# First layer: t1 and t6 turned into the score bank, and other places for copies, statistics, layer norm and loads

## The chip, the core and the metric

One Trainium2 chip, of which the kernel uses one core. The metric is the device time of one execution of the program in microseconds, the median of several executions. Names of the engines: PE is TensorE, DVE is VectorE, ACT is ScalarE, POOL is GpSimd, SP is SyncE, which only issues DMAs here.

## What is computed

Two layers over x, 128 rows of 256 tokens of 256 channels in f32. Each layer adds to x an attention over the 256 tokens of each row, on a group normalisation of its input. Cut to what matters:

```python
# layer 0
def _L0_conv_ref(x1d, x2d, norm_w, norm_b, qkv_w, x2d_w, gate_w, gate_b, final_w, final_b):
    c, h = 32, 8
    x = _layernorm(x1d, norm_w, norm_b)
    qkv = (x @ qkv_w.T).reshape(*x.shape[:-1], c, 3 * h)
    q, k, v = (qkv[..., :h], qkv[..., h:2 * h], qkv[..., 2 * h:])
    aff = jnp.einsum('bmich,bmjch->bmijh', q, k)
    gate = jax.nn.sigmoid(x @ gate_w.T + gate_b).reshape(*x.shape[:-1], c, h)
    bias = x2d @ x2d_w.T * (1.0 / math.sqrt(c))
    weights = jax.nn.softmax(aff + bias[:, None], axis=-2)
    out = jnp.einsum('bmrch,bmirh->bmich', v, weights) * gate
    return out.reshape(*x.shape[:-1], c * h) @ final_w.T + final_b
x = x + _L0_conv_ref(_gn(x), ...)      # _gn: group norm, 32 groups, over all rows and tokens
# layer 1: 4 heads of 64, only keys with |i - j| <= 16
x = x + _L1_conv_ref(_gn(x), ...)
```

## The kernel before

A prologue reads all of x once for the statistics of the first group norm (gstat0) and works out the pair bias for all rows (neg_bias). Then layer 0 runs row by row (`body0` of each engine), a second group norm follows (`group_norm(1, gstat1)`, from statistics of the rows' results), and layer 1 runs row by row (`body1`).

Each engine has its own program, written out by hand, in which the pieces of several rows stand between each other: m is the row whose softmax is finished, nxt = m + 1 the row whose projections are made, far = m + 2 the one whose normalised tokens are transposed, ahead = m + 3 the one whose tokens are scaled by the group norm, last = m - 1 the one whose heads are mixed with v, done = m - 2 the one whose result is added to x. There is no scheduler; the order of the calls in a body is the order on that engine, and semaphores tie the engines together. `over_rows` writes the first and last rows out and runs the rest in a loop of 4 rows an iteration.

A row of layer 0 on PE: the projections q, k, v and gate (12 matmuls each, since a product of f32 is made of three products of high and low parts), two groups of `scores` of four heads (24 each), eight `turns(h)` (four transposes each, of a head's 256 x 256 weights), `mixes` (32), the transposes of xn (L561), and the y projection (12). The four banks of `score` hold the scores of four heads at a time; `turn` is one bank. `turns(3)` and `turns(7)` go to the first score bank, the other six to `turn`, and each turn waits until the copy of the one before it in its bank is done.

A head's way: `scores` on PE; `mins` on DVE (L926) adds the bias and finds the row's minimum; `exps` on ACT (L722), with the sum; `inverse` on DVE (L932), for two heads at a time; `norms(r, j)` on POOL (L364) for heads 2j and 2j + 1, two instructions a head; `turns` on PE (L527); `turn_copy` to probT, on ACT (L728) for even heads, on DVE (L937) for odd ones; `mixes` on PE.

A row's tokens: SP loads x_tok (L329), POOL multiplies by the group norm's scale (L386, g_tok) and adds its shift (L392), DVE takes statistics (`bn_stats`, L1001, L1008) and ln_neg, ln_var (L1010, L1011), POOL works out ln_rstd, ln_off and xn (L370, L372, L377), PE transposes it, ACT writes xnT (L741) and the high part of src (L746), DVE its low part (`split_low`, L915: both inputs in SBUF). In the same way q, k and the attention's result have a high part from ACT (L732, L751, L757) and a low part from DVE (L952, L973, L981; the last has both inputs in SBUF). The result y is added to x on DVE (L948, y_sb) and stored by SP (L321). y_sb has two slots, and in every second row DVE takes `bn_stats` of both slots, for each of the two channel blocks (L1018).

## Time and profile before

| what | value |
|---|---|
| median of 3 runs | 3655.28 us (3653.41 to 3656.13) |
| profiled execution | 3664.15 us, its span 3662.3 us |
| PE / DVE / ACT / POOL busy over the span | 3372.3 / 3002.9 / 2776.3 / 2177.9 us |
| granted TensorE clock, mean | 0.969 |
| layer 0's loop | from about 250 to 2350 us |
| layer 1's loop | from about 2450 us to the end |

A busy time is a sum over stages with different limits, so the layer that the diff touches is read by itself. PEld is the weight load of each matmul; it has the clearer starts, and a piece's time is read from the start of its first weight load to the start of the next piece's. The other engines' operations overlap a little at their ends, so their pace too is read from start to start. Instructions with read-outs of accumulators stand beside `mins` and `exps` and overlap them.

### The profile page before, as it was taken

What the parts mean: (1) busy time and instruction counts of PE and PEld (TensorE: products, weight loads), DVE (VectorE), ACT (ScalarE), POOL (GpSimd) and SP (SyncE); (2) the same over time, 40 slices, a digit from 0 to 9 for tenths busy, and PEclk for the clock granted to TensorE, in tenths of its full rate; (3) what the DMA queues carried; (4) which work ended last, traced back from release to release, by engine and by line L of the source; (5) the groups of instructions that cost most, each with busy time, mean ns of one, the idle gap of its engine ahead of it and who ended that gap; (6) DMA issues with size and microseconds to landing.
All of it is one profiled execution on the core that took longest, in us unless ns stands there. A gap on an engine that the chain in (4) does not pass through costs nothing.

```text
span 3662.3 us, 122873 instructions
## 1 busy us (share of the span) xinstructions
PE 3372.3 (92%) x36747; PEld 3007.4 (82%) x36747; DVE 3002.9 (82%) x10850; ACT 2776.3 (76%) x8999; POOL 2177.9 (59%) x4107
## 2 busy tenths in 40 slices
PE   4459999999999999999999999799999999999999
PEld 1148888888888888888888888699999999999998
DVE  4458988888888888888888888688888888888887
ACT  1148888988888888888888988567667677776776
...
GB/s 341 349 100 54 46 49 51 44 52 45 50 52 43 52 46 48 52 43 52 46 48 50 44 52 44 30 53 52 52 52 52 52 53 54 53 52 52 52 52 47
DMA packets 189032, 238.42 MB, mean 65 GB/s; under 512 B 11824, under 2 KB 176176, under 8 KB 184752
## 3 DMA queue, kind: packets, MB, share of 16 engines
...
q8 instruction: 29, 0.48, 0.1%
...
## 4 chain that ended last, share of the span: by engine, by line
PE 58%; ACT 14%; issue 11%; DMA 6%; DVE 6%; POOL 2%; DVEq 1%; SPq 1%; ACTq 1%; POOLq 0%
PE work L477 24%; ACT prob L722 7%; PE work L486 7%; PE turn L527 5%; PE score L617 5%; PE mix L650 4%; DMA x_chunk<-xT 4%; PE mix L539 3%; PE score L505 3%; DMA x_tok<-x_nat 3%; PE turn L634 3%; ACT xnT L741 2%; ACT probT L728 2%; PE turn L635 2%; PE turn L636 2%
## 5 line engine op out<-in xcount | busy, mean ns | idle before, releaser
L364 POOL TENSOR_SCALAR prob<-prob,row_inv 128x256 f32<-128x256 f32 x2048 | 1068.0, 540 | 206.1 <-DVE row_inv L932 204.9
L722 ACT ACTIVATE prob<-prob,row_min 128x256 f32<-128x256 f32 x2048 | 1028.1, 507 | 128.3 <-DVE row_min L926 123.6
L477 PE MATMUL work<-src,w 128*128 128x256 f32 x7680 | 1067.5, 288 | 10.4 <-DVE src L915 6.7
L477 PEld LDWEIGHTS work<-src,w 128*128 128x128 f32 x7680 | 951.0, 189 | 12.3 <-DVE src L915 7.4
L415 POOL TENSOR_SCALAR prob<-prob,row_inv 128x160 f32<-128x160 f32 x1024 | 391.0, 401 | 767.4 <-DVE row_inv L1042 767.4
L926 DVE CUSTOM_DVE_ANT_0 prob<-score,neg_bias 128x256 f32<-128x256 f32 x2048 | 749.5, 417 | 17.2 <-PE score L505 10.1
L527 PE MATMUL turn<-ident,prob 128*128 128x128 f32 x3072 | 484.8, 280 | 120.0 <-ACT probT L728 101.4
L789 ACT ACTIVATE prob<-prob,row_min 128x160 f32<-128x160 f32 x1024 | 431.4, 426 | 141.7 <-DVE row_min L1035 141.6
L527 PEld LDWEIGHTS turn<-ident,prob 128*128 128x128 f32 x3072 | 336.3, 141 | 233.2 <-ACT probT L728 125.6
L477 PE MATMUL work<-att,wf 128*128 128x256 f32 x3072 | 432.1, 290 | 4.4 <-DVE att L981 3.0
L486 PE MATMUL work<-w,src 128*128 128x256 f32 x3072 | 425.8, 288 | 0.0
L722 ACT ACTIVATION_READ_ACCUMULATOR prob<-prob,row_min 128x1 f32 x2048 | 397.5, 194 | 0.0
L477 PEld LDWEIGHTS work<-att,wf 128*128 128x128 f32 x3072 | 385.0, 191 | 5.1 <-DVE att L981 3.5
L486 PEld LDWEIGHTS work<-w,src 128*128 128x128 f32 x3072 | 380.6, 189 | 0.1
L728 ACT COPY probT<-turn 128x512 f32<-128x512 f32 x512 | 297.2, 580 | 76.4 <-PE turn L527 69.8
L386 POOL TENSOR_TENSOR g_tok<-x_tok,gn_row 128x512 f32<-128x512 f32 x128 | 164.5, 1285 | 189.0 <-DMA x_tok<-x_nat 181.9
L1035 DVE CUSTOM_DVE_ANT_0 prob<-score,band 128x160 f32<-128x160 f32 x1024 | 263.3, 321 | 16.5 <-issue 2.4
L505 PE MATMUL score<-kT,nqT 32*128 32x256 f32 x6144 | 251.9, 294 | 6.1 <-DVE probT L937 3.2
L539 PE MATMUL mix<-probT,v_sb 128*32 128x256 f32 x4096 | 250.3, 385 | 0.0
L505 PEld LDWEIGHTS score<-kT,nqT 32*128 32x128 f32 x6144 | 199.7, 184 | 44.3 <-DVE probT L937 14.3
L932 DVE RECIPROCAL row_inv<-row_sum 128x4 f32<-128x4 f32 x512 | 90.2, 176 | 142.3 <-ACT prob L722 135.6
L1052 DVE SCALAR_TENSOR_TENSOR kT<-work,vec_sb,kT 128x256 fp32r<-128x256 f32 x256 | 112.1, 480 | 108.8 <-ACT kT L813 108.8
...
## 6 DMA issues: line engine op xcount, KB each, us to landing
...
x_tok<-x_nat SPq DMA_DIRECT2D x128, 256.0 KB, 3.3
x_sb<-xT SPq DMA_DIRECT2D x128, 256.0 KB, 3.4
x1T<-y_sb SPq DMA_DIRECT2D x128, 256.0 KB, 2.2
x_sb<-x1T SPq DMA_DIRECT2D x128, 256.0 KB, 2.9
outT<-y_sb SPq DMA_DIRECT2D x128, 256.0 KB, 2.2
...
```

Of the source, the lines that this page charges most:

```text
L364: pool.tensor_scalar(prob[:, h, ib], prob[:, h, ib], row_inv[:, h, ib:ib + 1], 1.0, ALU.mult, ALU.mult).then_inc(norm_done[0], 1)
L415: pool.tensor_scalar(w, w, row_inv1[:, r.base % 2, g, a, ib:ib + 1], 1.0, ALU.mult, ALU.mult).then_inc(norm_done[1], 1)
L477: ins = pe.matmul(out[:, cb], w[:, of_w, kb, cols + cb * P:cols + (cb + 1) * P], x[:, of_x, kb], start=n == 0, stop=n == len(terms) - 1)
L486: ins = pe.matmul(out[:, tb], x[:, of_x, kb, tb * P:(tb + 1) * P], w[:, of_w, kb, cols:cols + CH], start=n == 0, stop=n == len(terms) - 1)
L505: ins = pe.matmul(score[:, h, ib], nqT[q, r.base % 2, of_q, hg, ib * P:(ib + 1) * P], kT[q, r.base % 2, of_k, hg], start=n == 0, stop=n == ...
L527: ins = pe.transpose(to[:, jb * TOK + ib * P:jb * TOK + (ib + 1) * P], prob[:, h, ib, jb * P:(jb + 1) * P], ident[:])
L539: ins = pe.matmul(mix[h * D0:(h + 1) * D0, hg], v_sb[:, r.base % 2, jb, c:c + D0], probT[:, hg, h, jb], start=jb == 0, stop=jb == TB - 1, ...
L722: act.activation(prob[:, h, ib], prob[:, h, ib], ACT.Exp, bias=row_min[:, h, ib:ib + 1], scale=-1.0, accum_out=row_sum[:, h, ib:ib + 1]).t ...
L728: act.copy(probT[:, h // HPG, h % HPG].rearrange("p b t -> p (b t)"), turn[:]).then_inc(turn_done[0][0], 1)
L789: act.activation(w, w, ACT.Exp, bias=row_min1[:, m.base % 2, g, a, ib:ib + 1], scale=-1.0, accum_out=row_sum1[:, m.base % 2, g, a, ib:ib + ...
L926: dve.tensor_tensor_reduce(prob[:, h, ib], score[:, h % HPG, ib], neg_bias[:, ib, h], 1.0, 3.0e38, ALU.add, ALU.min, row_min[:, h, ib:ib + ...
L1035: dve.tensor_tensor_reduce(prob1[:, m.base % 2, g, a, ib * WIN:(ib + 1) * WIN], score[:, 2 * g + a, ib, 0:WIN], band[:, ib], 1.0, 3.0e38, ...
```

## The change

On each engine the same instructions are issued for a row, with the same sizes. What differs is the bank of two turns, the waits that follow from that, and the order.

- PE: turns 1, 3 and 6 go to the score bank, the others, 7 too, to `turn`. Turn 1 stands right behind turn 0, turn 6 behind turn 5 and ahead of the y projection. The waits in `turns` and `scores` follow.
- ACT: exponentials of head 5 right behind copy 0; those of heads 6, 7 and copy 4 ahead of the high part of att; the copy of v, the gate and copy 6 ahead of the next row's heads 0 to 2.
- DVE: the minima of head 7 behind the copy of turn 1; those of the next row's heads 0 and 1 ahead of att's low part, those of 2 and 3 and the inverse behind the statistics of g; copy 7 last. The statistics of y_sb are split: block 1 at the head of even rows, block 0 in the middle of odd ones, and the last one behind the loop.
- POOL: the norms of heads 4, 5 ahead of both operations on g; layer norm of row m + 3 at the end of the body, ahead of the norms of the next row's heads 0 and 1, in place of that of m + 2 at its start.
- SP: the load of x_tok ahead of the store of y and the load of x_sb.

The diff, cut to its core (waits of the moved pieces stay as they were, but for layer norm's far, which becomes ahead):

```diff
                     last, far, ahead = m + -1, m + 3, m + 4
+                    if n == 0 and ahead.exists:
+
+                        wait(sp, gn_scaled, ahead.times(1, -1))
+                        apart(sp, sp_passed)
+                        sp.dma_start(x_tok[:, ahead.base % 2], x_tok_v[:, bass.ds(ahead.times(TB), TB), :]
+                                     ).then_inc(x_tok_in[ahead.base % 2], 16)
                     if last.exists:
...
@@ -364,20 +364,9 @@
                             pool.tensor_scalar(prob[:, h, ib], prob[:, h, ib], row_inv[:, h, ib:ib + 1],
                                                1.0, ALU.mult, ALU.mult).then_inc(norm_done[0], 1)
...
-                if far.exists:
-                    wait(pool, ln_var_done, far.times(2, 2))
-                    apart(pool, pool_passed)
-                    pool.tensor_tensor(ln_rstd[:], ln_var[:], minus_half[:], ALU.pow).then_inc(ln_rstd_done, 1)
-                    wait(pool, ln_rstd_done, far.times(2, 1))
...
                 if m.exists:
                     norms(m, 1)
+                    norms(m, 2)
                 if ahead.exists:
 
                     wait(pool, x_tok_in[ahead.base % 2], ahead.times(16, 16, of=2))
...
                     pool.tensor_tensor(g, x_tok[:, ahead.base % 2], gn_row[:, 0].unsqueeze(1).broadcast_to([P, TB, CH]),
                                        ALU.mult).then_inc(gn_scaled, 1)
-                if m.exists:
-                    norms(m, 2)
-                if ahead.exists:
                     wait(pool, gn_scaled, ahead.times(1, 1))
                     pool.tensor_tensor(g, g, gn_row[:, 1].unsqueeze(1).broadcast_to([P, TB, CH]), ALU.add
                                        ).then_inc(g_done[0], 1)
                 if m.exists:
                     norms(m, 3)
+                if ahead.exists:
+                    wait(pool, ln_var_done, ahead.times(2, 2))
...
                 if nxt.exists:
                     norms(nxt, 0)
...
-                    wait(pe, turn_done[0][1], r.times(PAIRS0, 2 * hg - 2))
+                    if hg == 0:
+                        wait(pe, turn_done[0][1], r.times(PAIRS0, -2))
+                    else:
+                        wait(pe, turn_done[0][0], r.times(PAIRS0, 0))
...
                 def turns(h):
                     wait(pe, norm_done[0], m.times(TB * H0, TB * (h + 1)))
                     to = turn[:]
-                    if h % HPG == HPG - 1:
+                    if h in (1, 3, 6):
 
                         to = score[:, 0].rearrange("p b t -> p (b t)")
-                        if h < HPG:
-                            wait(pe, min_done[0], m.times(TB * H0, TB * (HPG + 1)))
-                        elif nxt.exists:
+                    if h == 0:
+                        wait(pe, turn_done[0][1], m.times(PAIRS0, 0))
+                    elif h == 1:
+                        wait(pe, min_done[0], m.times(TB * H0, TB * (HPG + 1)))
+                    elif h == 2:
+                        wait(pe, turn_done[0][0], m.times(PAIRS0, 1))
+                    elif h == 3:
+                        wait(pe, turn_done[0][1], m.times(PAIRS0, 1))
+                    elif h == 4:
+                        wait(pe, turn_done[0][0], m.times(PAIRS0, 2))
+                    elif h == 5:
+                        wait(pe, turn_done[0][0], m.times(PAIRS0, 3))
+                    elif h == 6:
+                        wait(pe, turn_done[0][1], m.times(PAIRS0, 2))
+                        if nxt.exists:
                             wait(pe, min_done[0], nxt.times(TB * H0, TB))
-                    elif h % HPG == 0:
-                        wait(pe, turn_done[0][0], m.times(PAIRS0, h // 2))
-                    elif h % HPG == 1:
-                        wait(pe, turn_done[0][0], m.times(PAIRS0, h // 2 + 1))
                     else:
-                        wait(pe, turn_done[0][1], m.times(PAIRS0, h // 2))
+                        wait(pe, turn_done[0][1], m.times(PAIRS0, 3))
...
                 if m.exists:
                     turns(0)
+                    turns(1)
                 if far.exists:
 
...
-                if m.exists:
-                    turns(1)
...
                 if m.exists:
                     turns(5)
+                    turns(6)
                 if last.exists:
...
                 if m.exists:
-                    turns(6)
                     turns(7)
...
                 if m.exists:
                     exps(m, 3)
                     exps(m, 4)
-                    turn_copy(0)
+                    turn_copy(0, turn[:])
+                    exps(m, 5)
                 if far.exists:
...
-                if m.exists:
-                    exps(m, 5)
                 if nxt.exists:
                     wait(act, k_ps[0], nxt.times(1, 1))
                     act.copy(kT[:, nxt.base % 2, HIGH], work[:, 0]).then_inc(k_high[0], 1)
                 if m.exists:
-                    turn_copy(2)
+                    turn_copy(2, turn[:])
+                    exps(m, 6)
+                    exps(m, 7)
+                    turn_copy(4, turn[:])
...
-                if m.exists:
-                    exps(m, 6)
...
-                if m.exists:
-                    exps(m, 7)
-                    turn_copy(4)
-                if nxt.exists:
-                    exps(nxt, 0)
...
+                if m.exists:
+                    turn_copy(6, score[:, 0].rearrange("p b t -> p (b t)"))
+                if nxt.exists:
+                    exps(nxt, 0)
                     exps(nxt, 1)
-                if m.exists:
-                    turn_copy(6)
-                if nxt.exists:
                     exps(nxt, 2)
...
+                def out_stats(ob, r, pair):
+                    wait(dve, y_done[0], r.times(1, 1))
+                    apart(dve, dve_passed)
+                    at = slice(pair, pair + 1) if isinstance(pair, int) else bass.ds(pair, 1)
+                    dve.bn_stats(gstat1[:, ob, at], y_sb[:, ob].rearrange("p r t -> p (r t)")).then_inc(y_stats, 1)
+
                 done = last + -1
                 if done.exists:
+                    if done.base % 2 == 0 and (done + -1).exists:
+                        out_stats(1, done + -1, done.times(1, -1, of=2))
...
@@ -956,7 +968,6 @@
                     inverse(m, 1)
                     mins(m, 5)
                     mins(m, 6)
-                    mins(m, 7)
                 if last.exists:
...
                 if m.exists:
-                    turn_copy(1, turn[:])
-                if m.exists:
+                    turn_copy(1, score[:, 0].rearrange("p b t -> p (b t)"))
+                    mins(m, 7)
                     inverse(m, 2)
+                if done.exists and done.base % 2 == 1:
+                    out_stats(0, done, done.times(1, 0, of=2))
...
@@ -976,23 +989,16 @@
                     turn_copy(3, score[:, 0].rearrange("p b t -> p (b t)"))
                 if far.exists:
                     split_low(0, far, xnT[:])
+                if nxt.exists:
+                    mins(nxt, 0)
+                if m.exists:
+                    inverse(m, 3)
+                if nxt.exists:
+                    mins(nxt, 1)
...
-                if nxt.exists:
-                    mins(nxt, 0)
-                if m.exists:
-                    inverse(m, 3)
-                if nxt.exists:
-                    mins(nxt, 1)
-                    mins(nxt, 2)
-                if m.exists:
-                    turn_copy(5, turn[:])
-                if nxt.exists:
-                    mins(nxt, 3)
-                if nxt.exists:
-                    inverse(nxt, 0)
                 if ahead.exists:
...
                 if m.exists:
-                    turn_copy(7, score[:, 0].rearrange("p b t -> p (b t)"))
+                    turn_copy(5, turn[:])
...
-                if done.exists and done.base % 2 == 1:
-                    wait(dve, y_done[0], done.times(1, 1))
-                    apart(dve, dve_passed)
-                    for ob in range(CB):
-                        pair = done.base // 2
-                        at = slice(pair, pair + 1) if done.loop is None else bass.ds(done.times(1, 0, of=2), 1)
-                        dve.bn_stats(gstat1[:, ob, at], y_sb[:, ob].rearrange("p r t -> p (r t)")).then_inc(y_stats, 1)
+                if nxt.exists:
+                    mins(nxt, 2)
+                    mins(nxt, 3)
+                    inverse(nxt, 0)
+                if m.exists:
+                    turn_copy(7, turn[:])
 
             over_rows(dve, 3, 2, body0)
 
+            dve.wait_ge(y_done[0], ROWS)
+            dve.bn_stats(gstat1[:, 1, ROWS // 2 - 1:ROWS // 2], y_sb[:, 1].rearrange("p r t -> p (r t)")).then_inc(y_stats, 1)
```

PE, one row of layer 0 in the written-out part: from turn 0 (the first turn below) to the k projection, and from turn 5 to the turn behind the y projection (`work<-att,wf`). Before:

```order
L527 MATMUL turn<-ident,prob 128x128 x4
L561 MATMUL work<-ident,xn 128x128 x4
L527 MATMUL turn<-ident,prob 128x128 x4
L477 MATMUL work<-src,w 128x256 x12
...
L527 MATMUL turn<-ident,prob 128x128 x4
L477 MATMUL work<-att,wf 128x256 x12
L527 MATMUL turn<-ident,prob 128x128 x4
L527 MATMUL score<-ident,prob 128x128 x4
```

After:

```order
L536 MATMUL turn<-ident,prob 128x128 x4
L536 MATMUL score<-ident,prob 128x128 x4
L571 MATMUL work<-ident,xn 128x128 x4
L475 MATMUL work<-src,w 128x256 x12
...
L536 MATMUL turn<-ident,prob 128x128 x4
L536 MATMUL score<-ident,prob 128x128 x4
L475 MATMUL work<-att,wf 128x256 x12
L536 MATMUL turn<-ident,prob 128x128 x4
```

The turn to the score bank now follows the first one at once, ahead of the transposes of xn; at the end one to the score bank has come ahead of the y projection, and one to `turn` stands behind it.

POOL, one row, from the norms of heads 2, 3 (the first `prob` row) to those of the next row's heads 0, 1 and what stands behind them. Before:

```order
L364 TENSOR_SCALAR prob<-prob,row_inv 128x256 x4
...
L386 TENSOR_TENSOR g_tok<-x_tok,gn_row 128x512
...
L364 TENSOR_SCALAR prob<-prob,row_inv 128x256 x4
...
L392 TENSOR_TENSOR g_tok<-g_tok,gn_row 128x512
...
L364 TENSOR_SCALAR prob<-prob,row_inv 128x256 x4
...
L364 TENSOR_SCALAR prob<-prob,row_inv 128x256 x4
...
L370 TENSOR_TENSOR ln_rstd<-ln_var,minus_half 128x2
...
L372 TENSOR_TENSOR ln_off<-ln_neg,ln_rstd 128x2
L377 TENSOR_SCALAR xn<-g_tok,ln_rstd,ln_off 128x256 x2
```

After:

```order
L364 TENSOR_SCALAR prob<-prob,row_inv 128x256 x4
...
L364 TENSOR_SCALAR prob<-prob,row_inv 128x256 x4
...
L375 TENSOR_TENSOR g_tok<-x_tok,gn_row 128x512
...
L378 TENSOR_TENSOR g_tok<-g_tok,gn_row 128x512
...
L364 TENSOR_SCALAR prob<-prob,row_inv 128x256 x4
...
L385 TENSOR_TENSOR ln_rstd<-ln_var,minus_half 128x2
...
L387 TENSOR_TENSOR ln_off<-ln_neg,ln_rstd 128x2
L392 TENSOR_SCALAR xn<-g_tok,ln_rstd,ln_off 128x256 x2
...
L364 TENSOR_SCALAR prob<-prob,row_inv 128x256 x4
```

The two `g_tok` rows stood one on either side of the norms of heads 4, 5 and are now neighbours behind them; the three rows of layer norm have moved ahead of the last norms.

DVE, where an even row begins: layer norm's last steps, statistics of y_sb (`gstat`), the addition that writes y_sb. Before:

```order
L937 COPY probT<-score 128x512
...
L1008 BN_AGGR ln_mv<-ln_st 128x2
...
L1008 BN_AGGR ln_mv<-ln_st 128x2
...
L1010 TENSOR_SCALAR ln_neg<-ln_mv 128x2
L1011 TENSOR_SCALAR ln_var<-ln_mv 128x2
...
L1018 BN_STATS gstat<-y_sb 128x6
...
L1018 BN_STATS gstat<-y_sb 128x6
...
L948 TENSOR_TENSOR y_sb<-work,x_sb 128x2x256
L952 TENSOR_TENSOR nqT<-work,nqT 128x512
L926 ISA prob,row_min<-score,neg_bias 128x256
```

After:

```order
L930 ISA prob,row_min<-score,neg_bias 128x256
...
L930 ISA prob,row_min<-score,neg_bias 128x256
...
L936 RECIPROCAL row_inv<-row_sum 128x4
L941 COPY probT<-turn 128x512
...
L948 BN_STATS gstat<-y_sb 128x6
...
L960 TENSOR_TENSOR y_sb<-work,x_sb 128x2x256
...
L964 TENSOR_TENSOR nqT<-work,nqT 128x512
```

Two statistics ahead of the addition have become one, and ahead of it stand the minima of the next row's head 3, an inverse and the copy of turn 7 where layer norm's steps stood.

## Rows read from the trace of the kernel before

**Rows 1.** Windows view: start:end, length, busy of PE, PEld, DVE, ACT, POOL; clock, DMA.

```profile
400.00:2200.00 1800.00, 1693.61 (x19380) 1489.32 (x19379) 1596.19 (x5842) 1591.17 (x4958) 1416.69 (x2424) 1.00 0.16 48
```

**Rows 2.** Source view of L732: count, min/median/max ns, first and last start.

```profile
L732 ACT CAST nqT<-work x119: 587/587/592, 308.3 to 2236.6; 128x512 fp32r<-128x512 f32 x119
```

**Rows 3.** The waits view, 300 to 2250 us: us in total, times, longest us.

```profile
POOL g_tok L386 <- DMA x_tok<-x_nat: 177.5, 119, 2.1
...
PEld turn L527 <- ACT probT L728: 125.1, 119, 1.6
...
PE turn L527 <- POOL prob L364: 9.6, 27, 0.7
```

**Rows 4.** Timeline, PE's weight loads: start, us, what, [idle before <-releaser].

```profile
1003.83 0.78 PEld L505 LDWEIGHTS score<-kT,nqT 32*128 32x128 f32 x24
...
1013.75 0.42 PEld L527 LDWEIGHTS turn<-ident,prob 128*128 128x128 f32 x4 [0.41 <-issue]
...
1015.16 0.42 PEld L527 LDWEIGHTS turn<-ident,prob 128*128 128x128 f32 x4 [0.55 <-ACT probT L728]
...
1019.53 0.77 PEld L505 LDWEIGHTS score<-kT,nqT 32*128 32x128 f32 x24 [0.24 <-DVE probT L937]
1020.44 0.42 PEld L527 LDWEIGHTS turn<-ident,prob 128*128 128x128 f32 x4
...
1022.68 1.50 PEld L477 LDWEIGHTS work<-att,wf 128*128 128x128 f32 x12
...
1029.47 0.42 PEld L527 LDWEIGHTS turn<-ident,prob 128*128 128x128 f32 x4 [0.41 <-issue]
...
1031.75 0.42 PEld L527 LDWEIGHTS turn<-ident,prob 128*128 128x128 f32 x4 [1.42 <-ACT probT L728]
...
1036.33 0.78 PEld L505 LDWEIGHTS score<-kT,nqT 32*128 32x128 f32 x24
```

**Rows 5.** The timeline of DVE over the head of the long row.

```profile
1025.12 0.75 DVE L1001 BATCH_NORM_STATS2 ln_st<-g_tok 128x6 f32<-128x256 f32 x2
...
1027.05 1.28 DVE L1018 BATCH_NORM_STATS2 gstat<-y_sb 128x512 f32 x2
1028.47 0.69 DVE L948 TENSOR_TENSOR y_sb<-work,x_sb 128x512 f32<-128x512 f32 x1
...
1029.68 0.41 DVE L926 CUSTOM_DVE_ANT_0 prob<-score,neg_bias 128x256 f32<-128x256 f32 x1
...
1030.36 0.17 DVE L932 RECIPROCAL row_inv<-row_sum 128x4 f32<-128x4 f32 x1
```

**Rows 6.** The timeline of ACT over the same two rows.

```profile
1014.52 0.59 ACT L728 COPY probT<-turn 128x512 f32<-128x512 f32 x1 [0.60 <-PE turn L527]
...
1018.53 0.62 ACT L757 CAST att<-att_sum 128x512 fp32r<-128x512 f32 x1
...
1030.14 0.51 ACT L722 ACTIVATE prob<-prob,row_min 128x256 f32<-128x256 f32 x1 [1.76 <-DVE row_min L926]
...
1031.13 0.56 ACT L728 COPY probT<-turn 128x512 f32<-128x512 f32 x1
```

**Rows 7.** The timeline of POOL over the same two rows.

```profile
1011.45 0.70 POOL L370 TENSOR_TENSOR ln_rstd<-ln_var,minus_half 128x2 f32<-128x2 f32 x1 [0.27 <-DVE ln_var L1011]
...
1012.66 1.09 POOL L377 TENSOR_SCALAR xn<-g_tok,ln_rstd,ln_off 128x256 f32<-128x256 f32 x2 [0.24 <-POOL ln_off L372]
...
1018.38 2.79 POOL L364 TENSOR_SCALAR prob<-prob,row_inv 128x256 f32<-128x256 f32 x4
...
1030.74 1.84 POOL L364 TENSOR_SCALAR prob<-prob,row_inv 128x256 f32<-128x256 f32 x4 [1.05 <-DVE row_inv L932]
```

**Rows 8.** The timelines of POOL and DVE where operations of both meet.

```profile
253.56 1.28 POOL L392 TENSOR_TENSOR g_tok<-g_tok,gn_row 128x512 f32<-128x512 f32 x1
...
253.90 1.50 DVE L915 TENSOR_TENSOR src<-xnT,src 128x512 fp32r<-128x512 f32 x1
...
1068.51 0.99 POOL L364 TENSOR_SCALAR prob<-prob,row_inv 128x256 f32<-128x256 f32 x1
```

34 lines of the change are left out of this document (16 added, 18 removed).

## The prediction

> **What bounds the kernel now.** First the windows: in the first layer's steady part PE is busy 94%, DVE 89%, ACT 88%, POOL 79%, at a granted clock of 1.00 [rows 1]. Four engines that full, in fixed orders, are bound by their waits for each other more than by one engine's sum. Second, the spacing of one ACT instruction that comes once a row: 119 of them from 308.3 to 2236.6 us, 16.34 us a row [rows 2]. Third, who waited: PE 125.1 us for ACT's copy of a turn, once a row, in front of turn 1; POOL 177.5 us for the load of x_tok; PE only 9.6 us for POOL's normalised heads [rows 3]. Fourth, PE's weight loads of two rows. I write S0 for the first scores of the next row, t0 to t7 for the turns, m4 to m7 for the minima of the row's heads, n0 to n3 for those of the next row, and nq low, src low, att low for DVE's low parts. From S0 to S0 it takes 15.70 us if the row ends at 1019.53 and 16.80 us if it ends at 1036.33; the wait before t1 is 0.55 in the one and 1.42 in the other [rows 4]. The two read here make 32.50; the mean pair is 32.68, since long rows vary. The reason for the long one is on DVE: in every second row two batch statistics of y_sb (1.28), and y_sb's wait behind them, put m4 late, at 1029.68; ACT idles 1.76 us before exponentials 4, and the copy of t0 behind these starts at 1031.13 in place of 1030.24 (t0's start plus 0.77, the distance in the short row) [rows 4 to 6].
>
> **What the change removes.** (1) t1 goes to the score bank and stands right behind t0, so its wait for ACT's copy goes (0.55 and 1.42), and t2 no longer needs DVE's copy of t1. (2) The two statistics no longer stand together: in odd rows one comes in the middle, where DVE would wait for ACT's kT, and costs nothing (0.60 if that wait were gone); in even rows one stays at the head. (3) The load of x_tok is issued as soon as its buffer is read, ahead of the store of y: POOL's wait, 1.5 a row, goes. The store loses nothing, since it waits for a later event. (4) Layer norm on POOL moves ahead of the norms of the next row's heads 0 and 1: 2.3 us (1011.45 to 1013.75) [rows 7], then 1.85. By the places below these heads are ready 0.3 to 0.9 before t0 and t1, so it costs nothing.
>
> **What is late next in an odd row.** That t1 doesn't wait helps only if S0 can come earlier. S0 waits for copy 3, which stands behind kT's low part, which waits for ACT's kT; and between copy 0 and kT ACT does what it did before: exponentials 5, xnT, src, in another order. In the short row copy 0 starts at 1014.52 and S0 at 1019.53, 5.01 later. PE needs 9.92 from S0 to t0 (1003.83 to 1013.75; the same operations stand between them after the change), and copy 0 comes 0.77 behind t0 [rows 4, 6]. 9.92 + 0.77 + 5.01 is **15.70**, what a short row takes now. The 0.55 turns into a wait before S0, and an undisturbed row gains nothing.
>
> **What is late next in an even row.** Here the chain over DVE is longer. From the S0 before: t4 0.91 later, ACT's copy 4 after 0.77, it and att high 0.59 and 0.62 long with 0.1 of overlap, 0.04 to DVE's start: att low at 2.82. In the new order there follow att low 0.60 (an operation of 512 columns takes that from start to start: y_sb and nq low 1.21 from 1028.47 to 1029.68); statistics of g, copy 5 and the small ones of layer norm 1.93 (1025.12 to 1027.05); n2 and n3 at 0.68 each; an inverse 0.10; copy 7 0.60; a statistic and y_sb's wait behind it 0.82 (two and the wait take 1.42 now, the first 0.60); y_sb and nq low 1.21. That puts m4 at 9.44. Then 0.46 to exponentials 4, 0.99 to copy 0, 5.01 to S0: **15.90** [rows 4 to 6]. DVE and ACT alone would so give 31.60 for two rows, against 32.68.
>
> **The new wait.** t6 now stands ahead of the y projection, where that stands today, 3.15 behind S0 (1022.68) [rows 4]. It needs head 6 normalised, and on POOL both operations on g now stand between the norms of heads 4, 5 and those of 6, 7. In the even row m4, inverse, m5, m6, att_sum, copy 1 and m7 (4 x 0.68 + 0.10 + 1.20) put inverse 2 at S0 - 2.44. The norms start 0.38 later (1030.36 to 1030.74 [rows 5, 7]) and take 1.85, to S0 - 0.21. Scaling g takes 1.28, to 1.07; adding the shift the same, behind a wait for its predecessor's result that the norms hid until now (xn waits 0.24 so [rows 7]; I take 0.1), to 2.45; two norms 0.93 and 0.07 to PE: 3.45, so t6 would wait 0.3.
>
> To this comes contention. A norm of POOL over which DVE's src low ran took 0.99 for 0.48; two DVE operations with both inputs in SBUF in a row, src low and att low, make four norms last 2.79 for 1.85; and once src low, issued inside a g addition of 1.28, took 1.50 for 0.68: it waited until that addition ended [rows 7, 8]. In the new order src low is issued 0.14 before S0, in the very moment at which the scaling of g starts, and att low 2.8 to 3.1 behind it, as the norms for t6 start. Today both fall on norms of heads 4 and 5, where t4 has time. Each costs POOL 0.45 to 0.5, so head 6 comes at 4.4 and **t6 waits 1.3**. The bounds: 0.3 with no contention, 1.6 with both and DVE's own delay passed on. In the odd row inverse 2 is 0.5 earlier and t6 waits 0.2 to 0.4, which the next row's DVE chain hides; att low, held up there by a norm, adds 0.28 to that chain.
>
> The Trainium skill (SBUF — State Buffer, "SBUF: two separate sides") says that GpSimd and a DVE operation with two SBUF inputs share a pair of ports as an exclusive lock, held for a whole instruction. By that rule src low may be held up for a whole operation on g at each meeting, which speaks against putting the two behind each other here; by the 0.99 alone it would cost a norm's length, and t6 would wait 0.8. The one long row agrees with the rule.
>
> **Sum.** Odd to even 15.90 + 0.28 = 16.18; even to odd 15.70 + 1.3 = 17.00; two rows 33.18. Now they take 32.68. The difference of 0.50 times 62 pairs is +31 us. Around the loop stands one more statistic ahead of the second group norm, +0.7. The second layer's loop is untouched. The profiled execution ran 3664.2 us, 9 above the median of 3655.3; differences go on the median: **3687 us**.
>
> **Rivals.** (a) *The operations don't meet.* Phases that differ by 0.3 us from mine put src low and att low beside a waiting POOL. Then t6 waits 0.3, two rows take 31.9, and 62 x -0.78 gives -48 us: **3607**. For it: POOL idles in every row today; against it: the new order has work behind work in just this stretch. (b) *One of the two meets*: t6 waits 0.8, two rows take 31.60 + 0.1 + 0.8 and the 0.18 by which long rows vary now, 32.68: no change, **3655**. (c) *DVE is held up behind the scaling of g in odd rows too*: n0, n1, att low and all of the chain of 15.90 come 0.4 later, in both rows, two rows take 34.0, +80, **3735**. It decides from the point where src low is issued after the scaling has begun. (d) *The change doesn't do what it says*: excluded by the order, in which t0 and t1, and the two operations on g, are neighbours.
>
> **How the numbers follow.** Forecast 0.45, (c) 0.07, (b) 0.17, (a) 0.31. So slower than +0.2% (about what a measurement of this kernel can tell from no change) 0.52; within 0.2% 0.17; faster 0.31. The range starts at 3610, which cuts off less than half of (a), and goes to 3716: the forecast with t6's wait at 1.6 and half of (c)'s delay. Some 0.1 to 0.15 is left out below, 0.08 above. The forecast's own range is 3668 to 3709.
>
> **What would show it.** Right: PE's wait for ACT in front of t1 gone; a wait for POOL's normalised heads in front of t6 of about 1 us in every second row, 60 to 100 us in all against 9.6; S0 waiting for copy 3 in nearly every row; POOL's wait for x_tok gone; src low with instances over 1 us; rows of 16.2 and 17.0. Wrong: t6 waits little and rows take 15.9, then the contention was mis-sized; if rows take 15.7 throughout, the chain of 15.90 was wrong too; below that, the 5.01 from copy 0 to S0 was. The granted clock should stay 1.00.

## The result, and the profile after

The changed kernel takes **3666.0 us** in the median (3662.7 to 3673.6) against 3655.6 of the kernel before on the same chip: a ratio of 1.0028, 95% interval 1.0017 to 1.0039, so slower by 0.28% or 10.4 us. Forecast were 3687 us and slower. The sign came as forecast and the time lies in the range, but the loss is a third of the 31.7 us of the sum: 3687 was wrong in size.

The profiled execution took 3663.5 us (span 3661.7), no longer than the one of before. That is not the loop's doing: layer 0's first row began 7 us earlier in it (its first nqT at 225.2 us against 232.4), so the loops are compared by their pace and not by the spans. First the windows view over the stretch of [rows 1], then the source view of the instruction of [rows 2]:

```profile
400.00:2200.00 1800.00, 1669.57 (x19305) 1477.20 (x19298) 1613.80 (x5804) 1580.55 (x4932) 1383.43 (x2413) 1.00 0.16 48
```

```profile
L740 ACT CAST nqT<-work x119: 561/568/579, 301.5 to 2239.2; 128x512 fp32r<-128x512 f32 x119
```

The clock is 1.00 as before. The 119 starts lie from 301.5 to 2239.2 us, 16.42 us a row against 16.34: 0.08 us over some 125 rows is the 10 us. From its first nqT to its last, layer 0 takes 2087.1 us in the one profile and 2076.9 in the other, layer 1 takes 1274.5 and 1274.7: the result lies in layer 0's loop.

Third, the waits view, 300 to 2250 us (us in total, times, longest us), to be read against [rows 3]:

```profile
POOL prob L364 <- DVE row_inv L936: 308.8, 275, 1.7
...
PEld score L506 <- DVE probT L941: 106.6, 119, 1.1
...
PE score L506 <- DVE probT L941: 83.2, 119, 0.9
PEld score L536 <- issue: 82.9, 118, 1.0
...
ACT prob L730 <- DVE row_min L930: 57.9, 60, 1.0
PE score L536 <- POOL prob L364: 57.4, 88, 0.8
DVE row_inv L936 <- ACT prob L730: 55.8, 89, 0.7
```

What the change took away is gone: no wait for x_tok (177.5 us before), none in front of turn 1 (125.1 before), and ACT's wait for minima, 118.3 us before, is half. Two waits of PE stand in their place. The scores, `score L506`, wait for DVE's copy of turn 3 in every row, 119 times. The turns into the score bank, `score L536`, wait 118 times, nearly always turn 6; the weight load's share is put down to "issue", PE's own to POOL's norms. Fourth, PE's weight loads over the two rows from the S0 of 999.54 (start, us, what, [idle before <-releaser]), against [rows 4]:

```profile
1003.75 0.42 PEld L536 LDWEIGHTS score<-ident,prob 128*128 128x128 f32 x4 [1.02 <-issue]
...
1010.34 0.42 PEld L536 LDWEIGHTS turn<-ident,prob 128*128 128x128 f32 x4 [0.41 <-issue]
1010.73 0.47 PEld L536 LDWEIGHTS score<-ident,prob 128*128 128x128 f32 x4
...
1016.10 0.77 PEld L506 LDWEIGHTS score<-kT,nqT 32*128 32x128 f32 x24 [0.76 <-DVE probT L941]
...
1019.96 0.42 PEld L536 LDWEIGHTS score<-ident,prob 128*128 128x128 f32 x4 [0.67 <-issue]
1020.34 1.49 PEld L475 LDWEIGHTS work<-att,wf 128*128 128x128 f32 x12
...
1026.55 0.42 PEld L536 LDWEIGHTS turn<-ident,prob 128*128 128x128 f32 x4 [0.41 <-issue]
...
1032.65 0.78 PEld L506 LDWEIGHTS score<-kT,nqT 32*128 32x128 f32 x24 [1.06 <-DVE probT L941]
```

t0 and t1 stand together at 1010.34 and 1010.73; t1 waits for nothing, t0 no longer than before (0.41). t6 waits at 1003.75 and 1019.96, S0 at 1016.10 and 1032.65. The pattern repeats every four rows. The next table is worked out from the starts of all weight loads from 300 to 2250 us: the mean from one piece's start to the next, less what the same piece takes where it doesn't wait (0.43 from t5 to t6, 1.60 from the v projection to S0). Class 0 and 2 lead from an even row's S0 to an odd one's, 1 and 3 back.

| class | t6 waits | S0 waits | S0 to S0 | forecast |
|---|---|---|---|---|
| 0 | 0.99 | 0.61 | 16.53 | 17.00 |
| 1 | 0.20 | 0.84 | 16.03 | 16.18 |
| 2 | 1.06 | 0.61 | 16.59 | 17.00 |
| 3 | 0.70 | 0.92 | 16.56 | 16.18 |

A mean row waits 0.74 us for t6 and 0.74 for S0. Without both it would take 14.94 (an estimate: 16.42 less the two, with no other wait in their place). The room is there, and the change uses none of it.

What lies behind these waits stands on DVE and POOL. The timeline of DVE, from the end of one row to the first minima of the next:

```profile
1015.97 1.14 DVE L919 TENSOR_TENSOR src<-xnT,src 128x512 fp32r<-128x512 f32 x1
1017.32 0.42 DVE L930 CUSTOM_DVE_ANT_0 prob<-score,neg_bias 128x256 f32<-128x256 f32 x1 [0.21 <-PE score L506]
...
1023.24 0.18 DVE L936 RECIPROCAL row_inv<-row_sum 128x4 f32<-128x4 f32 x1 [0.57 <-ACT prob L730]
1023.34 0.68 DVE L941 COPY probT<-turn 128x512 f32<-128x512 f32 x1
1024.10 0.69 DVE L948 BATCH_NORM_STATS2 gstat<-y_sb 128x512 f32 x1
1024.93 0.69 DVE L960 TENSOR_TENSOR y_sb<-work,x_sb 128x512 f32<-128x512 f32 x1
...
1026.14 0.41 DVE L930 CUSTOM_DVE_ANT_0 prob<-score,neg_bias 128x256 f32<-128x256 f32 x1
...
1031.92 0.68 DVE L941 COPY probT<-score 128x512 f32<-128x512 f32 x1
1032.51 1.65 DVE L919 TENSOR_TENSOR src<-xnT,src 128x512 fp32r<-128x512 f32 x1
...
1034.78 0.17 DVE L936 RECIPROCAL row_inv<-row_sum 128x4 f32<-128x4 f32 x1
```

and of POOL there:

```profile
1032.33 1.29 POOL L375 TENSOR_TENSOR g_tok<-x_tok,gn_row 128x512 f32<-128x512 f32 x1
1033.70 1.63 POOL L378 TENSOR_TENSOR g_tok<-g_tok,gn_row 128x512 f32<-128x512 f32 x1
1035.31 1.81 POOL L364 TENSOR_SCALAR prob<-prob,row_inv 128x256 f32<-128x256 f32 x3
```

src low (`src<-xnT,src`) takes 1.14 and 1.65 us where its neighbour, a copy of the same 512 columns, takes 0.68. The 1.65 end at 1034.16, which is 0.54 behind the end of the scaling of g (1032.33 + 1.29 = 1033.62): src low, issued 0.18 after that began, did nearly all of its work behind it. POOL's next one, the addition of the shift, lasts 1.63 for 1.28. How regular this is shows the source view of src low (min/median/max ns), before and after:

```profile
L915 DVE TENSOR_TENSOR src<-xnT,src x120: 681/704/1022, 300.6 to 2246.0; 128x512 fp32r<-128x512 f32 x120
```

```profile
L919 DVE TENSOR_TENSOR src<-xnT,src x119: 1090/1643/1732, 309.7 to 2247.6; 128x512 fp32r<-128x512 f32 x119
```

Before, the longest of 120 is 1.02 us. After, the shortest of 119 is 1.09.

### The profile page after: what moved, and what is told of

It reads as the page before. It is cut to its first block, busy times and chain, and to the rows that moved or that the text cites. A ratio compares the mean times of both kernels' runs of the same rounds, so it can differ in the third digit from the quotient of the medians.

```text
span 3661.7 us, 123057 instructions
## 1 busy us (share of the span) xinstructions
PE 3352.4 (92%) x36747; PEld 3001.4 (82%) x36747; DVE 3030.4 (83%) x10850; ACT 2772.9 (76%) x8999; POOL 2145.8 (59%) x4107
## 4 chain that ended last, share of the span: by engine, by line
PE 47%; DVE 15%; POOL 14%; issue 13%; ACT 6%; DMA 3%; DVEq 1%; ACTq 1%; POOLq 0%; SPq 0%
PE work L475 18%; POOL prob L364 7%; DVE prob L930 5%; PE work L484 5%; PE score L625 5%; PE mix L658 4%; POOL g_tok L378 4%; ACT prob L730 3%; POOL g_tok L375 3%; DMA x_chunk<-xT 3%; PE turn L642 3%; DVE probT L941 2%; PE mix L548 2%; PE score L506 2%; PE score L536 2%
## 5 line engine op out<-in xcount | busy, mean ns | idle before, releaser
L364 POOL TENSOR_SCALAR prob<-prob,row_inv 128x256 f32<-128x256 f32 x2048 | 998.4, 506 | 351.7 <-DVE row_inv L936 344.3
L536 PE MATMUL turn<-ident,prob 128*128 128x128 f32 x2560 | 398.3, 278 | 3.8 <-POOL prob L364 2.9
L536 PEld LDWEIGHTS turn<-ident,prob 128*128 128x128 f32 x2560 | 284.4, 140 | 74.1 <-issue 38.7
L506 PE MATMUL score<-kT,nqT 32*128 32x256 f32 x6144 | 252.2, 294 | 87.3 <-DVE probT L941 87.0
L736 ACT COPY probT<-turn 128x512 f32<-128x512 f32 x384 | 224.3, 584 | 109.3 <-PE turn L536 109.3
L506 PEld LDWEIGHTS score<-kT,nqT 32*128 32x128 f32 x6144 | 200.0, 184 | 129.1 <-DVE probT L941 107.4
L536 PE MATMUL score<-ident,prob 128*128 128x128 f32 x1536 | 238.1, 278 | 64.3 <-POOL prob L364 62.9
L536 PEld LDWEIGHTS score<-ident,prob 128*128 128x128 f32 x1536 | 173.4, 141 | 92.4 <-issue 84.9
L378 POOL TENSOR_TENSOR g_tok<-g_tok,gn_row 128x512 f32<-128x512 f32 x128 | 206.7, 1615 | 10.0
```

What stands on the lines that cost most here:

```text
L364: pool.tensor_scalar(prob[:, h, ib], prob[:, h, ib], row_inv[:, h, ib:ib + 1], 1.0, ALU.mult, ALU.mult).then_inc(norm_done[0], 1)
L378: pool.tensor_tensor(g, g, gn_row[:, 1].unsqueeze(1).broadcast_to([P, TB, CH]), ALU.add).then_inc(g_done[0], 1)
L506: ins = pe.matmul(score[:, h, ib], nqT[q, r.base % 2, of_q, hg, ib * P:(ib + 1) * P], kT[q, r.base % 2, of_k, hg], start=n == 0, stop=n == ...
L536: ins = pe.transpose(to[:, jb * TOK + ib * P:jb * TOK + (ib + 1) * P], prob[:, h, ib, jb * P:(jb + 1) * P], ident[:])
```

## The experiments

Twelve kernels ran. Three causes were on trial for t6's wait: both operations on g standing ahead of head 6's norms (the prediction's), t6's place ahead of the y projection, and src low held up by an operation on g. Each edit is against the kernel after, unless the text says another. The kernels ran on chips on which the one before took 3648.1 us (e1 to e4), 3655.3 (e5 to e8) and 3656.3 (e9 to e12), so the ratios are to be compared, not the times.

### Is it the two operations on g, or t6's place?

**e1** puts the scaling of g back ahead of the norms of heads 4 and 5, so that one operation on g stands before head 6 and not two.

```diff
                 if m.exists:
                     norms(m, 1)
-                    norms(m, 2)
...
                     pool.tensor_tensor(g, x_tok[:, ahead.base % 2], gn_row[:, 0]...,
                                        ALU.mult).then_inc(gn_scaled, 1)
+                if m.exists:
+                    norms(m, 2)
+                if ahead.exists:
                     wait(pool, gn_scaled, ahead.times(1, 1))
```

> The changed kernel with one edit on POOL: the scaling of g goes back ahead of the norms of heads 4 and 5, the addition of the shift stays behind them (the load of x_tok stays early). Theory A (t6 waits for head 6 because both operations on g stand between the norms of 4, 5 and 6, 7): PE's wait in front of t6, 0.74 us a row now, falls under 0.2, the pair of rows takes 31.6 in place of 32.85, and the time falls by about 75 us, to 3590. Rival B (what t6 gives back goes into the wait in front of S0, since the chain from copy 0 sets the row): S0's wait grows by what t6's loses, rows stay at 16.4, time within 10 us of 3666.

Measured: 3658.8 us, ratio 1.0035 (1.0021 to 1.0049). No gain; t6 waits 0.72 in the mean. The time is rival B's, but not for B's reason: S0's wait stays at 0.74. **e3** leaves both operations in their place, but does the addition on one column a block:

```diff
-                    pool.tensor_tensor(g, g, gn_row[:, 1].unsqueeze(1)..., ALU.add
+                    pool.tensor_tensor(g[:, :, 0:1], g[:, :, 0:1], gn_row[:, 1, 0:1].unsqueeze(1)..., ALU.add
```

> The changed kernel with the shift of g added to one column of each token block only (the rest of the addition is left out, so POOL has 1.2 us less to do a row between the same norms). Theory A: as e1 or a little less time, 3585 to 3600, the wait in front of t6 under 0.2. Rival B: within 10 us of 3666.

Measured: 3656.8 us, ratio 1.0029 (1.0016 to 1.0042). The addition takes 0.52 us for 1.63, and little comes sooner; t6 waits 0.89, 0.20, 0.95 and 0.70 in the four classes. In classes 0 and 2 of the kernel after head 6's norms start 2.66 and 2.73 behind S0, right behind the addition; in e3 they start at 2.49 and 2.57, and in e1 at 2.51 and 2.59. So POOL's work ahead of head 6 is the last to come by 0.15 only, and something else stands right behind it. The timelines of DVE and of POOL in e1 say what does:

```profile
1032.31 1.67 DVE L921 TENSOR_TENSOR src<-xnT,src 128x512 fp32r<-128x512 f32 x1
...
1034.58 0.17 DVE L938 RECIPROCAL row_inv<-row_sum 128x4 f32<-128x4 f32 x1
...
1035.35 0.69 DVE L1002 TENSOR_TENSOR att<-att_sum,att 128x512 fp32r<-128x512 f32 x1
```

```profile
1032.13 1.29 POOL L380 TENSOR_TENSOR g_tok<-g_tok,gn_row 128x512 f32<-128x512 f32 x1
1034.96 1.43 POOL L364 TENSOR_SCALAR prob<-prob,row_inv 128x256 f32<-128x256 f32 x2 [1.53 <-DVE row_inv L938]
```

src low is held up as long as before (1.67), now behind the addition of the shift, which has moved into the place of the scaling. POOL has long been free, for 1.53 us, when the inverse comes at 1034.58, 2.13 behind S0 (1032.45), and head 6's norms can start. POOL's work got shorter, and the inverse, which stands behind src low on DVE, became the wait. A second thing hangs on it: att low starts at 1035.35, ahead of head 6's second norm, which starts at 1035.41 and takes 0.98 for 0.48. The two norms of 1.43 in the row above are 0.49 and 0.98.

**e2** puts t6 back behind the y projection, with POOL's order as in the kernel after.

```diff
                     turns(5)
-                    turns(6)
...
                     project(work[:, 1], wf0, 0, att).then_inc(y_ps[0], 1)
                 if m.exists:
+                    turns(6)
                     turns(7)
```

> The changed kernel with turn 6 put back behind the y projection, in its new bank; nothing else. Theory A: PE's wait in front of t6 goes, but t6 itself comes no earlier (4.6 us behind S0 against 4.2 now), so copy 6, the next exponentials of ACT, nqT and with them copy 0 come later: rows stay at 16.3 to 16.5, time 3650 to 3675. Rival C (the place of t6 is the fault): rows fall to 15.8, time 3590.

Measured: 3797.4 us, ratio 1.0405 (1.0387 to 1.0423), which neither theory had. The waits view, 300 to 2250 us:

```profile
ACT probT L736 <- PE score L536: 217.3, 112, 2.0
...
PEld score L536 <- DVE row_min L930: 100.1, 111, 1.4
```

t6's place is no error of the change. ACT stands in front of copy 6, with the exponentials of the next row's heads 0 to 2 queued behind it, and loses 217 us there; t1, which waits for the minima of m4 in its bank, waits in its turn (99 of the 100.1 us). With the copies in the new order t6 must be early.

### Is it src low?

**e5** makes both operations on g one column wide, so that src low meets next to nothing. It leaves the rest of the scaling and the shift out; g_tok holds a constant, set once at the start.

```diff
-                    pool.tensor_tensor(g, x_tok[:, ahead.base % 2], gn_row[:, 0]..., ALU.mult
+                    pool.tensor_tensor(g[:, :, 0:1], x_tok[:, ahead.base % 2, :, 0:1], gn_row[:, 0, 0:1]..., ALU.mult
...
-                    pool.tensor_tensor(g, g, gn_row[:, 1]..., ALU.add
+                    pool.tensor_tensor(g[:, :, 0:1], g[:, :, 0:1], gn_row[:, 1, 0:1]..., ALU.add
```

**e6** (against e1) takes src low out of the meeting instead: on DVE it stands behind the minima of the next row's head 1.

```diff
-                if far.exists:
-                    split_low(0, far, xnT[:])
                 if nxt.exists:
                     mins(nxt, 0)
...
                     mins(nxt, 1)
+                if far.exists:
+                    split_low(0, far, xnT[:])
```

**e9** (against e1) changes no place at all. It adds a wait on POOL, so that the addition of the shift starts only when src low is done:

```diff
                     wait(pool, gn_scaled, ahead.times(1, 1))
+                    wait(pool, src_done[0], far.times(1, 1))
                     pool.tensor_tensor(g, g, gn_row[:, 1]..., ALU.add
```

> The changed kernel with both operations on g cut to one column of each token block (the rest of the scaling and of the shift is left out; g_tok is set to a constant once at the start). With the shift alone cut, t6 still waited, and src low still took 1.7 us for 0.68 behind the scaling. Theory D (what is left of t6's wait comes from DVE: src low is held up behind whichever operation on g is under way, so the minima of the next row's head 0 and inverse 3 come late): src low takes 0.68 to 0.9, inverse 3 comes 1.7 us behind S0 in place of 2.2, t6 waits 0.1 to 0.4 (0.74 now), two rows 32.0 in place of 32.85, time 3605 to 3620. Rival B (what t6 gives back goes into S0's wait): within 10 us of 3666.

> The order of the run with the scaling ahead of the norms of 4 and 5, with one more edit on DVE: src low stands behind the minima of the next row's heads 0 and 1, so it no longer meets an operation on g, but a norm of heads 6, 7, as att low behind it does. Theory D: inverse 3 comes 1.7 us behind S0, but the norms for t6 lose 0.5 to 1.0 to the two; t6 waits 0.3 to 0.9; DVE's chain gets 0.3 longer; two rows 32.3 to 32.7, time 3635 to 3660. Rival B: 3655 to 3670.

> The order of the run with the scaling ahead of the norms of 4 and 5, with one wait more: POOL adds the shift to g only when src low of the row is done. It takes no work away; it only keeps the two apart. Theory D (src low, held up behind the addition of the shift, makes inverse 3 and t6 late): src low takes 0.68 in all rows, inverse 3 comes 1.9 us behind S0 in place of 2.2, head 6 0.3 earlier in even rows; t6 waits 0.5 a row in place of 0.77, time 3625 to 3645 against 3658.8. Rival (the addition, 0.8 later, is what t6 waits for, or the wait costs what the lock did): 3650 to 3670.

Measured: e5 3626.3 us, ratio 0.9924 (0.9904 to 0.9943); e6 3717.9 us, 1.0171 (1.0154 to 1.0188); e9 3625.2 us, **0.9912** (0.9897 to 0.9927). e9 is in the range that its expectation named; e5 is 6 us above its own, and e6 58 us above. e9 does all of the work and takes 1.2% less than the kernel after, as much as e5 with nearly no operation on g. Its source view of src low, and DVE and POOL around the S0 of 1025.56:

```profile
L922 DVE TENSOR_TENSOR src<-xnT,src x121: 679/682/683, 299.4 to 2233.1; 128x512 fp32r<-128x512 f32 x121
```

```profile
1025.43 0.68 DVE L922 TENSOR_TENSOR src<-xnT,src 128x512 fp32r<-128x512 f32 x1
...
1027.48 0.17 DVE L939 RECIPROCAL row_inv<-row_sum 128x4 f32<-128x4 f32 x1
...
1028.47 0.86 DVE L1003 TENSOR_TENSOR att<-att_sum,att 128x512 fp32r<-128x512 f32 x1 [0.15 <-ACT att L770]
```

```profile
1026.19 1.28 POOL L381 TENSOR_TENSOR g_tok<-g_tok,gn_row 128x512 f32<-128x512 f32 x1 [0.92 <-DVE src L922]
1027.86 1.82 POOL L364 TENSOR_SCALAR prob<-prob,row_inv 128x256 f32<-128x256 f32 x3 [0.39 <-DVE row_inv L939]
```

All 121 src low take 0.68. POOL waits 0.92 for them, the inverse comes 1.92 behind S0 in place of 2.13, head 6's norms start 2.30 behind it in place of 2.51, and t6 waits 0.39 in the mean, not 0.72. S0's wait stays at 0.75. That is what src low's hold cost: 1.2% between e1 and e9, one wait apart. That the addition of the shift starts later isn't the reason: in e5 nothing starts later, the two operations are only short, and it gains as much. The gain falls in classes 0 and 2 (16.43 and 16.52 to 15.82 and 16.03 in the mean); in 1 and 3 src low's hold of about 1.1 us ended before the minima could start anyway, and nearly all of their rows stay at 16.05 and 16.57.

The 0.21 by which the norms start sooner is the smaller part of that: t6 comes 0.7 sooner in class 0. The rest is the second meeting. In e1 head 6's second norm starts at 1035.41, behind att low's start at 1035.35, and takes 0.98. In e9 it starts at 1028.32, ahead of att low's at 1028.47, and takes 0.48; att low takes 0.86. In classes 0 and 2 att low catches this norm in 58 of 59 rows of e1 and in 14 of 60 of e9 (all 14 in class 2, where t6 then waits 0.74, and 0.21 otherwise).

e6 has src low at 0.69 and the inverse just as early (1.92), and is slower than all but e2. Its DVE and POOL, around the S0 of 1032.23:

```profile
1034.90 0.69 DVE L921 TENSOR_TENSOR src<-xnT,src 128x512 fp32r<-128x512 f32 x1
1035.51 0.68 DVE L1002 TENSOR_TENSOR att<-att_sum,att 128x512 fp32r<-128x512 f32 x1
```

```profile
1034.53 2.84 POOL L364 TENSOR_SCALAR prob<-prob,row_inv 128x256 f32<-128x256 f32 x4 [1.82 <-DVE row_inv L938]
```

Four norms take 2.84 for 1.84: src low and att low, back to back, hold POOL inside head 6, which costs it two holds in one norm (1.47 for 0.48), and t6 waits 1.2 us in every row. So it isn't enough that src low isn't held up; it matters which of POOL's operations the low parts meet. The Trainium skill (SBUF — State Buffer, "SBUF: two separate sides") describes the ports that GpSimd shares with such DVE operations as an exclusive lock held for a whole instruction; e9 (0.68 in all 121 rows once the two are in order) and e6 (1.47 for 0.48 behind two) agree with it, and e9 shows what ordering the two is worth in this kernel, 1.2%.

### The parts done alone

**e4** is the kernel before with only the statistics of y_sb apart. **e8** is the kernel before with only t1 in the score bank behind t0 (its waits follow). **e11** is e8 with exponentials of head 5 behind copy 0, as the change has them.

```diff
 (e4)
                 if done.exists:
+                    if done.base % 2 == 0 and (done + -1).exists:
+                        out_stats(1, done + -1, done.times(1, -1, of=2))
...
                     inverse(m, 2)
+                if done.exists and done.base % 2 == 1:
+                    out_stats(0, done, done.times(1, 0, of=2))
 (e8)
-                    if h % HPG == HPG - 1:
+                    if h in (1, 3, 7):
...
                 if m.exists:
                     turns(0)
+                    turns(1)
...
-                if m.exists:
-                    turns(1)
 (e11, against e8)
                     turn_copy(0)
+                    exps(m, 5)
...
-                if m.exists:
-                    exps(m, 5)
```

> The kernel before with one part of the change alone: the two statistics of y_sb apart, one at the head of even rows, one behind inverse 2 in odd rows. My step for this part: the long rows lose 0.60 us, short ones nothing: -38 us, 3618. Rival: the statistics were hidden, as the wait moves elsewhere: within 7 us of 3655.6.

> The kernel before with one part of the change alone: turn 1 goes to the score bank and stands right behind turn 0. My step for this part: t1's wait for ACT's copy goes (0.55 and 1.42 a row), the same time is waited in front of S0, rows stay at 15.7 and 16.9: 3645 to 3660, no change. Rival (the wait was on the path): 0.5 us a row, 3590.

> The kernel before with turn 1 paired (3670.7 alone, slower) and the exponentials of head 5 moved behind copy 0 on ACT. Reading of that run: ACT waits 0.3 us in short rows between copy 0 and xnT, since the transposes of xn now stand behind turn 1; the exponentials fill that gap. Expected: copy 0 to S0 back to 5.0 us, short rows 15.8 in place of 16.3, time 3640 to 3658. Rival (the loss of that run came from t4 waiting for POOL): stays at 3665 to 3675.

Measured: e4 3657.0 us, 1.0023 (1.0012 to 1.0034); e8 3670.7 us, 1.0046 (1.0030 to 1.0062); e11 3656.9 us, 1.0001 (0.9991 to 1.0011). None gains. e11 is in the range that its expectation named; e4 was to gain 38 us, and e8 to change nothing. In e4 the long rows fall from 16.84 to 16.70 and the short ones rise from 15.86 to 16.10. DVE in a short row:

```profile
1017.89 0.18 DVE L932 RECIPROCAL row_inv<-row_sum 128x4 f32<-128x4 f32 x1 [1.17 <-ACT prob L722]
1018.13 0.70 DVE L944 BATCH_NORM_STATS2 gstat<-y_sb 128x512 f32 x1
1018.74 0.68 DVE L983 TENSOR_TENSOR kT<-work,kT 128x512 fp32r<-128x512 f32 x1
```

and its copy of k's high part on ACT:

```profile
1017.76 0.56 ACT L751 CAST kT<-work 128x512 fp32r<-128x512 f32 x1
```

The statistic "in the middle, where DVE would wait for ACT's kT" has no such gap here: inverse 2 waits 1.17 for exponentials 5, the statistic starts right behind it, and kT's low part, whose input ACT has ready at 1018.32, starts at 1018.74. Only with exponentials 5 earlier, as the change has them, is the gap there: 111.3 us in 119 waits in front of kT's low part in the kernel after. In e8 the wait in front of t1 goes, and the projection in front of S0 takes 2.53 for 1.69 in the short rows: ACT now waits for the transposes of xn, which come behind t1, and its copy of kT is later. The timeline of ACT:

```profile
1012.13 0.57 ACT L744 ACTIVATE xnT<-work,vec_sb 128x256 f32<-128x256 f32 x1 [0.22 <-PE work L566]
```

In the long rows t1, now in the bank of the scores, waits for the minima of m4 instead (43 of the 50.7 us that the turns into the score bank wait for minima). e11 gives the 0.3 of the short rows back, and no more. In both the 0.55 in front of t1 shows up in front of S0, as the prediction said.

### What is late in front of S0

S0 waits for copy 3, behind kT's low part, behind ACT's kT, and ACT's kT stands behind ACT's src. **e7** (against e1) and **e12** (against the kernel after) put kT ahead of src on ACT; src has a row's time. **e10** is e7 with e9's wait.

```diff
-                    wait(act, xnT_done, far.times(CB, CB))
-                    wait(act, gate_ps, far.times(1, -1))
-                    act.copy(src[:, far.base % 2, HIGH], xnT[:]).then_inc(src_high[0], 1)
                 if nxt.exists:
                     wait(act, k_ps[0], nxt.times(1, 1))
                     act.copy(kT[:, nxt.base % 2, HIGH], work[:, 0]).then_inc(k_high[0], 1)
+                if far.exists:
+                    wait(act, xnT_done, far.times(CB, CB))
+                    wait(act, gate_ps, far.times(1, -1))
+                    act.copy(src[:, far.base % 2, HIGH], xnT[:]).then_inc(src_high[0], 1)
```

> The order of the run with the scaling ahead of the norms of 4 and 5, with one edit on ACT: the high part of kT ahead of that of src. It shortens the chain from copy 0 to S0 (5.05) by 0.5. My step for odd rows (S0 is set by copy 0, exponentials, xnT, src, kT, kT low, copy 3): S0 comes 0.4 to 0.5 earlier in every row, the wait in front of S0 falls from 0.74 to 0.3 a row, and src low, now behind it, meets the norms of 4, 5 or the addition's start less, so t6's wait does not grow: rows 15.5 to 15.9, time 3550 to 3600. Rival (t6's wait takes it up, since inverse 3 is what the row hangs on): rows 16.3, 3650.

> The changed kernel with kT's high part ahead of src's on ACT and nothing else. If the gain of 105 us over the changed kernel is the shorter chain from copy 0 to S0 alone, this takes 3560 to 3585. If it needs the scaling of g ahead of the norms of 4 and 5 (S0 earlier means that head 6 has to be ready earlier, and POOL is 1.3 us behind), t6 waits 1 us or more in every row and it takes 3610 to 3640.

> The fastest run so far (kT's high part ahead of src's, 3561.7) with the same wait more: POOL adds the shift only when src low is done. There the two meet in every second row only (src low 1.71 us, t6 waits 0.96; in the other rows 0.68 and 0.22). Theory D: t6's wait falls to about 0.5 in those rows, 0.3 to 0.5 us in two rows: 3530 to 3550. Rival: within 10 us of 3562.

Measured:

| kernel | us | ratio (95%) | us a row | t6 waits | S0 waits |
|---|---|---|---|---|---|
| after | 3666.0 | 1.0028 (1.0017 to 1.0039) | 16.42 | 0.74 | 0.74 |
| e1 | 3658.8 | 1.0035 (1.0021 to 1.0049) | 16.41 | 0.72 | 0.74 |
| e9, e1 and the wait | 3625.2 | 0.9912 (0.9897 to 0.9927) | 16.11 | 0.39 | 0.75 |
| e12, after and kT ahead | 3667.7 | 1.0029 (1.0018 to 1.0041) | 16.48 | 1.48 | 0.1 |
| e7, e1 and kT ahead | 3561.7 | 0.9746 (0.9728 to 0.9764) | 15.66 | 0.57 | 0.1 |
| e10, all three | **3534.7** | **0.9668** (0.9654 to 0.9682) | 15.42 | 0.35 | 0.1 |

e12 misses its expectation and tells the most: its second case has what t6 does right (1 us or more in every row), but with a time 28 us too low. S0's wait goes as it should, and t6's doubles; the waits view, 300 to 2250 us:

```profile
PEld score L536 <- issue: 170.2, 118, 1.8
...
PE score L536 <- POOL prob L364: 142.8, 118, 1.6
```

POOL's part (norms of heads 4 and 5, scaling, shift, norms of 6) is released by inverse 2 and not by S0. With S0 0.6 us earlier t6 is asked for 0.6 earlier, and head 6 isn't. e1's order starts the scaling ahead of the wait for inverse 2, in time that POOL otherwise idles; alone that gave nothing, since the inverse behind src low was later anyway. e1 alone: 0. e12's edit alone: 0. Both (e7): 2.8% below the kernel after. With the wait (e10): 3.3% below the kernel before.

e7 and e10 are in the ranges that their expectations named. In e10 three classes take 15.2 to 15.4 and one 15.9, in which t6 still waits 0.7. The timelines of DVE and POOL, first in a row of the quick kind, then in the slow one, give the reason:

```profile
1015.41 0.95 DVE L1004 TENSOR_TENSOR att<-att_sum,att 128x512 fp32r<-128x512 f32 x1
```

```profile
1015.35 0.48 POOL L364 TENSOR_SCALAR prob<-prob,row_inv 128x256 f32<-128x256 f32 x1
```

```profile
1030.50 0.72 DVE L1004 TENSOR_TENSOR att<-att_sum,att 128x512 fp32r<-128x512 f32 x1
```

```profile
1030.51 0.98 POOL L364 TENSOR_SCALAR prob<-prob,row_inv 128x256 f32<-128x256 f32 x1
```

Head 6's second norm and att low start within 0.06 us of each other in both. Where the norm is first it takes 0.48, and att low 0.95; where att low is first it takes 0.72, and the norm 0.98. A few hundredths decide about 0.5 us of t6. The same happens in the kernel after: classes 1 and 3 differ in att low starting 2.82 or 2.75 behind S0, and the norm taking 0.48 or 0.98.

## Where the prediction was right and where wrong

The mechanism of the loss in even-to-odd rows, t6 waiting for head 6 while the low parts hold POOL up, was right. What failed are sizes in the sum: t6's wait (1.3, measured 1.0) and the base of an even-to-odd row (15.70, measured 15.55) make such a row 0.44 too long; odd to even is 0.12 longer than forecast (16.29 in the mean of classes 1 and 3, against 16.18). A pair so takes 32.84 and not 33.18, and 0.34 in 62 pairs is the 21 us by which the forecast was too high. That the change is slower at all is in part luck: with the two sizes put right the sum gives 32.74 a pair, 4 us above the kernel before (an estimate), and the rest comes from class 3, in the step that the prediction called hidden. What stands behind each follows.

**What the change removes: right.** The waits for x_tok and in front of t1 are gone, ln stands behind the norms without a cost to t0 and t1, and the store loses nothing that a row shows. "Costs nothing" for the statistic in the middle is right in this change and wrong for the edit by itself (e4): its cover, a wait for kT, is there only because exponentials 5 moved.

**The 0.55 turns into a wait before S0: right, one term too large.** S0 waits in all rows, copy 0 to S0 is 4.98 to 5.05 against the 5.01 used. The 9.92 from S0 to t0 held 0.15 of waits that the new order doesn't have; the pieces without waits add up to 9.77. So the base of an even-to-odd row is 15.55, not 15.70.

**t6's new wait: found, a third too large.** Forecast 1.3, measured 1.0. On POOL the scaling starts 0.25 to 0.32 before S0 (forecast 0.21), the shift 1.04 to 1.11 behind it (1.17), nearly as worked out. But src low's meeting costs POOL 0.34 (the 1.63 for 1.29), not 0.5, and att low's 0.43 and not 0.45 to 0.5, so that head 6 is done at 4.01 to 4.09 and not 4.4. 15.55 + 1.0 gives the 16.53 to 16.59 measured; 15.70 + 1.3 gave 17.00.

**Odd to even: the chain over DVE right, its cover wrong.** In class 1 the chain is as worked out, m4 at 9.60 against 9.44 and S0 at 16.03 against 15.90 to 16.18. In class 3 the step that failed is "t6 waits 0.2 to 0.4, which the next row's DVE chain hides". It waits 0.70, because att low catches head 6's second norm, and the chain passes it on: copy 6 later on ACT, the exponentials of heads 0 and 1 behind it, DVE's inverse waits for them (the 0.57 at 1023.24; 55.8 us in 89 waits), then copy 7, the statistic and y_sb, and m4 comes at 10.04. The row takes 16.56.

**The cause was only half named.** The prediction put the meeting with src low to POOL's account and named DVE's delay as rival (c), which "decides from the point where src low is issued after the scaling has begun". It is issued 0.1 to 0.2 us after in classes 0 and 2, and 0.7 after in the others, so (c)'s condition held in every row and its price did not: (c) asked 0.4 of delay for the chain and 80 us. The delay is real (up to 1.05) and sits in front of the next row's first minima, which wait for PE's scores anyway where the hold is short (0.21 at 1017.32, behind 1.14); where it is long the inverse comes 2.13 to 2.19 behind S0 and not 1.92, and no more. e1 and e3 show that taking an operation on g away from in front of head 6 is worth 0.1 of t6's wait and no time that the ratios show, since the inverse stands right behind; e9 shows that in e1's order src low's hold was the limit. That wait in the order of the kernel after was not run. So the number was too high while its mechanism was too narrow: without the hold on DVE, which the sum left out, e1's order runs 0.9% below the kernel before.

**The rivals.** (a), the operations don't meet, 3607, is what e5 and e9 bring about: 3626 and 3625. In e9 the pair of classes 0 and 1 takes 31.86, against (a)'s 31.9; the pair of 2 and 3 takes 32.60, since att low still catches head 6's second norm there. (b) and (d) didn't occur: in even-to-odd rows of the kernel after both low parts hold POOL up. PE's clock stayed 1.00.
